# Starting the third layer before the feed-forward layer has finished its last groups

## The reference, cut to what matters

```
x = x + conv_0(group_norm(x)); x = x + conv_1(group_norm(x))
t = tokens(x)                              # 16 images x 256 tokens x 96 channels
t = t + causal_attention_2(layer_norm(t))  # "layer 2": 6 heads of 16
t = t + bit_ffn(layer_norm(t))             # two sign-weight matmuls, 96 -> 384 -> 96
t = t + causal_attention_3(layer_norm(t))  # "layer 3", with biases
t = t + mixture_of_experts(layer_norm(t))  # 4 experts, top 2
```

## Time and profile before

| | us |
|---|---|
| median of 3 runs | 800.56 (797.04 to 800.75) |
| the profiled execution | 800.84 |
| its span | 798.6 |

### The profile page before, as it was taken

One profiled execution on the slowest core, in us unless ns is written; L12 is line 12 of the kernel. 1 busy time (PEld: TensorE's weight loads), 2 busy tenths in 40 slices (PEclk: granted clock), 3 DMA queues, 4 the chain that ended last, 5 costly groups with the idle time before them and its releaser, 6 DMA issues.

```text
span 798.6 us, 16946 instructions
## 1 busy us (share of the span) xinstructions
PE 739.9 (93%) x5265; PEld 579.9 (73%) x5265; DVE 582.8 (73%) x1415; ACT 570.7 (71%) x1425; POOL 252.8 (32%) x485
## 2 busy tenths in 40 slices
PE   1896999999999888999998987899999999999997
PEld 1874788787788776777776586677777787777775
DVE  6238677676777566888787698688887836988885
ACT  3323787877777556888887775688888847787785
POOL 1902255565554342122121100031221210534434
PEclk9999999999999999999999998899999989999999
DMA  6000000110110132323331002133233102322220
GB/s 219 1 1 0 1 7 17 21 16 17 21 16 16 24 91 66 101 81 104 91 92 29 0 1 69 52 97 103 79 104 92 41 1 55 78 65 74 60 50 21
DMA packets 60073, 41.36 MB, mean 52 GB/s; under 512 B 33904, under 2 KB 52464, under 8 KB 59888
## 3 DMA queue, kind: packets, MB, share of 16 engines
q1 hardware_dynamic: 60016, 40.63, 20.0%
HBM read 12.24 MB, written 3.21 MB: 19 GB/s over the span
## 4 chain that ended last, share of the span: by engine, by line
PE 78%; DVE 11%; ACT 4%; issue 3%; DMA 2%; SPq 1%; POOL 1%; POOLq 0%; DVEq 0%
PE ps L1248 11%; PE ps L992 10%; PE ps L1426 8%; PE ps L1183 8%; PE ps L1093 6%; PE ps L997 5%; PE ps L1077 3%; PE ps L1021 3%; PE ps L1035 3%; PE ps L1000 2%; PE ps L1022 2%; PE ps L942 2%; DVE amax L1867 2%; PE ps L1065 2%; DMA qk<-hl 1%
## 5 line engine op out<-in xcount | busy, mean ns | idle before, releaser
L627 ACT ACTIVATE ee<-ps,nmax 128x128 f32<-128x128 f32 (+1 forms) x576 | 204.7, 444 | 11.6 <-DVE nmax L1597 6.4
L1248 PE MATMUL ps<-w,ee 128*128 128x128 f32 x960 | 134.4, 273 | 2.0 <-ACT big L614 1.9
L1248 PEld LDWEIGHTS ps<-w,ee 128*128 128x128 f32 x960 | 112.4, 142 | 13.6 <-ACT ee L627 2.8
L614 ACT ACTIVATE big<-ps 128x512 f32<-128x512 f32 (+1 forms) x192 | 96.5, 554 | 24.3 <-PE ps L1248 22.4
L1600 DVE TENSOR_REDUCE nmax<-ps 128x2 f32<-128x256 f32 x192 | 97.5, 550 | 13.1 <-PE ps L1000 8.5
L1721 DVE TENSOR_TENSOR hhl<-ee,hhl 128x512 fp32r<-128x512 f32 x96 | 77.3, 815 | 26.2 <-ACT hhl L861 24.7
L992 PE MATMUL ps<-kh,big 128*128 128x256 f32 x384 | 94.7, 391 | 1.5 <-POOL big L387 1.2
L1597 DVE TENSOR_REDUCE nmax<-ps 128x4 f32<-128x1024 f32 x48 | 58.7, 1224 | 45.0 <-PE ps L992 44.8
L1426 PE MATMUL ps<-hhl,w2hl 128*96 128x512 f32 x288 | 83.3, 399 | 2.1 <-issue 1.8
L1183 PE MATMUL ps<-qk,w1hl 128*128 128x512 f32 x288 | 84.4, 402 | 0.0
L531 POOL TENSOR_TENSOR xc<-big,xc 96x512 f32<-96x512 f32 x32 | 52.9, 1655 | 95.2 <-DVE big L1952 94.6
(11 more groups left out here) (260 smaller groups left out, 1331.0 us busy)
## 6 DMA issues: line engine op xcount, KB each, us to landing
qk<-hl SPq DMA_DIRECT2D x256, 96.0 KB, 3.1
big<-moe_gate SPq DMA_DIRECT2D x8, 768.0 KB, 6.9
w<-w_in SPq DMA_DIRECT2D x1, 1735.0 KB, 12.3
xc<-x_in SPq DMA_DIRECT2D x4, 384.0 KB, 5.6
l_mix<-on SPq DMA_DIRECT2D x32, 48.0 KB, 2.1
tok<-l_mix SPq DMA_DIRECT2D x16, 96.0 KB, 2.0
out<-xc SPq DMA_DIRECT2D x8, 192.0 KB, 2.1
w<-w_in SPq DMA_DIRECT2D x1, 998.0 KB, 8.8
```

The source lines that it names most:

```text
L614: nc.scalar.activation(et[:, h, 0:w], ps[:, 4 + hh, 0:w], ACT.Copy).then_inc(own(l, f"et{hh}"), 1)
L627: last = nc.scalar.activation(ee[:, ke, hh, qc, 0:w], src, ACT.Exp, bias=nmax[:, kp, hh, qc:qc + 1])
L1248: last = nc.tensor.transpose(ps[:, 4 + hh, b * P:(b + 1) * P], ee[:, u, hh, qc, tc * P:(tc + 1) * P], ident)
```

## The change

- The lists are cut. `F2_PE`, `F2_ACT` and `F2_DVE` end earlier; what is left of groups 2, 3 and 4 moves into layer 3's written-out units, by tables: `F2_LATE_PE` (transposes 2 to 7 in units 0, 1, 5, 8, 11, 14), `F2_LATE_ACT` (their copies in the same units; roots 3, 4; normalising of groups 2, 3 in units 0 and 3), `F2_LATE_DVE` (`f` of groups 3 and 4 in units 0 and 1, `b` of group 3, `n` of group 4). POOL gets its own list, `F2_POOL`, with its maxima in the same order.
- Transposes and their copies no longer go by group in two halves but by four tiles (two images), T0 to T7, all into bank 6 (the first into bank 0), and layer 3 waits for each where it needs it: units 3, 6, 9, 12, 15 hold the weighing until a copy is done. POOL's staging and its other weights are put in a new order.
- On TensorE, `Q0` no longer follows all of the third group's matmul, `S0` waits for no later group's sums, and `Y2_BANKS` gives the second matmul ten uses of eight banks, so that groups 2 and 3 wait for no sum.
- Image 0's stacking is shared: SyncE issues four of its eight DMAs, ScalarE the other four (step `D0`).
- Layers 2 and 3 both lose the dummy image: for image -1 each step is only an increment of its semaphore. The matmuls L1194 and L1327 go too.
- In layer 3 six images are written out instead of two; the loop starts at image 6.

```diff
-F2_PE = [..., "y3", "T0", "Q0", "y4", "T1", "Q1", "S0", "T2", "S1", "T3", "V0", "T4"]
-F2_ACT = [..., "L0", "R0", "N0", "R1", "C0", "N1", "Q0", "R2", "N2", "C1", "Q1", "R3", "N3", "C2", "R4", "X0", "C3", "C4"]
-F2_DVE = [..., "y2", "b1", "f2", "k0", "y3", "b2", "f3", "y4", "k1", "b3", "m0", "f4", "n4", "m1", "v0"]
-Y2_BANKS = [(6, 7), (0, 1), (6, 2), (0, 1), (6, 2)]
+F2_PE = [..., "y3", "T0", "Q0", "y4", "Q1", "S0", "T1", "S1", "V0"]
+F2_ACT = [..., "L0", "R0", "N0", "C0", "Q0", "R1", "D0", "N1", "Q1", "R2", "X0", "C1"]
+F2_DVE = [..., "y2", "k0", "b1", "f2", "y3", "m0", "k1", "b2", "y4", "m1", "v0"]
+F2_LATE_PE = {0: [2], 1: [3], 5: [4], 8: [5], 11: [6], 14: [7]}
+F2_LATE_ACT = {0: ["C2", "N2"], 1: ["C3", "R3"], 2: ["R4"], 3: ["N3"], 5: ["C4"], 8: ["C5"], 11: ["C6"], 14: ["C7"]}
+F2_LATE_DVE = {0: ["f3"], 1: ["f4"], 2: ["b3"], 3: ["n4"]}
+Y2_BANKS = [(6, 7), (0, 1), (2, 3), (4, 5), (6, 3)]
...
-            def ln3_transposes(g):
+            def ln3_transposes(m):
+                g = (2 * m + 1) // GI
...
+                if m == 0:
+                    pe.wait_ge(sg("f2_y2"), 4)
+                elif m == 1:
+                    pe.wait_ge(sg("f2_y2"), 2 * NG)
+                else:
+                    pe.wait_ge(sg("l3_xn"), m)
+                for t in range(4):
+                    last = nc.tensor.transpose(ps[0:C, ln3_bank(m), t * P:(t + 1) * P], on[:, 4 * m + t, :], ident)
+                last.then_inc(sg("ln3_t_ps"), 1)
...
+                        elif step[0] == "D":
+                            act.wait_ge(*upto(3, "hi", g + 1))
+                            for t, (h0, h1) in enumerate(((0, 0), (0, 1), (1, 0), (1, 1))):
+                                if t == 1:
+                                    act.wait_ge(*upto(3, "lo", g + 1))
+                                parts = hl[C // 2:C, g, :, :, :].rearrange("c a h x -> c (a h) x")[:, h0:h1 + 3:h1 + 2 - h0, :]
+                                nc.scalar.dma_start(qk[(4 + t) * HD:(5 + t) * HD, g, 3:9, :].bitcast(F32), parts.bitcast(F32)).then_inc(own(3, f"stacked{g}"), 16)
...
@@ TensorE, unit @@
+                    if l == 3 and isinstance(k, int) and k in (3, 6, 9, 12, 15):
+                        pe.wait_ge(sg("l3_xn"), k // 3 + 3)
...
-                        weigh_values(l, npar, 0)
-                        weigh_values(l, npar, 1).then_inc(own(l, "av"), 1)
+                        if isinstance(i, int) and i == 0:
+                            pe.sem_inc(own(l, "av"), 1)
+                        else:
+                            weigh_values(l, npar, 0)
+                            weigh_values(l, npar, 1).then_inc(own(l, "av"), 1)
...
+                    if l == 3 and isinstance(k, int):
+                        for m in F2_LATE_PE.get(k, []):
+                            ln3_transposes(m)
...
-                for i in range(B if l == 1 else 2):
+                for i in range((0, B, 2, 6)[l]):
...
@@ VectorE, unit @@
+                    if l == 3 and isinstance(k, int):
+                        for step in F2_LATE_DVE.get(k, []):
+                            feed_step(step)
@@ TensorE, second matmul @@
-                                if g >= 2:
-                                    pe.wait_ge(sg("f2_y2"), 2 * (g - 2) + b + 1)
+                                if g == NG - 1:
+                                    pe.wait_ge(sg("f2_y2"), 1 if b == 0 else 6)
```

More of the change, by code:

```diff
@@ L307, in stack @@
                     parts = hl[:, par, :, :, :].rearrange("c a h x -> c (a h) x")[:, h0:h1 + 3:h1 + 2 - h0, :]
-                    for hh in range(2):
+                    for hh in sides:
                         r0 = hh * 4 * HD + t * HD
@@ L320, in _ @@
             for l in (2, 3):
-                stack(l, 0, 0)
-                stack(l, 1, 1)
+                for n in range(2):
+                    stack(l, n, n, (0,) if l == 3 and n == 0 else (0, 1))
                 if l == 2:
@@ L660, in outputs_to_sbuf @@
             def outputs_to_sbuf(l, i):
+                if isinstance(i, int) and i < 0:
+                    act.sem_inc(own(l, "ot"), 1)
+                    return
                 act.wait_ge(*upto(l, "av", i + 2))
@@ L670, in outputs_by_channel @@
             def outputs_by_channel(l, i):
+                if isinstance(i, int) and i < 0:
+                    act.sem_inc(own(l, "oc"), 1)
+                    return
                 act.wait_ge(*upto(l, "oc_ps", i + 2))
@@ L736, in inverse_root, with late @@
                     nc.scalar.activation(rs, rs, ACT.Exp, scale=-0.5).then_inc(sg("l1_rs"), 1)
+            def late(k):
+                for step in F2_LATE_ACT.get(k, []):
+                    g = int(step[1:])
+                    if step[0] == "R":
+                        ln3_root(g)
+                    elif step[0] == "N":
+                        ln3_norm(g)
+                    else:
+                        ln3_channels(g)
             for l in (1, 2, 3):
@@ L1038, in outputs @@
             def outputs(l, i):
+                if isinstance(i, int) and i < 0:
+                    pe.sem_inc(own(l, "oq"), 1)
+                    return
                 pe.wait_ge(*upto(l, "ot", i + 2))
@@ L1047, in outputs_back @@
             def outputs_back(l, i):
+                if isinstance(i, int) and i < 0:
+                    pe.sem_inc(own(l, "oc_ps"), 1)
+                    return
                 pe.wait_ge(*upto(l, "on", i + 2))
@@ L1061, in project_outputs @@
             def project_outputs(l, i):
+                if isinstance(i, int) and i < 0:
+                    pe.sem_inc(own(l, "out_ps"), 1)
+                    return
                 pe.wait_ge(*upto(l, "oc", i + 2))
@@ L1631, in normalise_outputs @@
             def normalise_outputs(l, i):
+                if isinstance(i, int) and i < 0:
+                    dve.sem_inc(own(l, "orec"), 1)
+                    dve.sem_inc(own(l, "on"), 1)
+                    return
                 dve.wait_ge(*upto(l, "oq", i + 2))
@@ L1641, in add_outputs @@
             def add_outputs(l, i):
+                if isinstance(i, int) and i < 0:
+                    dve.sem_inc(own(l, "added"), 1)
+                    return
                 dve.wait_ge(*upto(l, "out_ps", i + 2))
@@ L1907, in _ @@
+                    for step in F2_DVE:
+                        feed_step(step)
             dve.wait_ge(sg("f3_gl_ps"), 8)
```

193 lines of the change are left out of this document (97 added, 96 removed).

## The result

| | before | after |
|---|---|---|
| median, same chip | 799.51 (796.37 to 802.67, 20 runs) | 803.54 (799.17 to 806.68, 20 runs) |
| the profiled execution, its span | 800.84, 798.6 | 804.32, 802.4 |

The ratio is 1.0046, 95% interval [1.0031, 1.0061]: 3.7 us slower (the medians differ by 4.0). The forecast was 798.0, with a range up to 801.8. One kernel's time goes with its clock: of the 20 executions after, the three shortest (799.2 to 799.5) have a mean granted clock of 0.972 to 0.977, the three longest (806.1 to 806.7) 0.962 to 0.964.

The account below looks back on a forecast made before the run. TensorE bounds layer 3, DVE is late in the seam before it. Gains 8.5 - 2.0 - 1.3 = 5.2, less 3.0 for the clock, plus 0.5 in layer 2, make 2.7 off: 798 (797.9), range 794.8 to 801.8.

Parts of the forecast that it names:

- Step 1: Group 3's second matmul follows group 2's directly, with no sum to wait for, ending about 477.4; nothing uses this alone.
- Step 2: Image 0's path from transposes through DMAs shared by two issuing engines: scores 0 at 488.7, before 495.38.
- Steps 3 and 4: DVE's queue up to image 0's weighing, with `f4` at 3.8: weighing 0 at 507.4 instead of 515.94, 8.5 gained.
- Step 5: Image 1, with group 3's normalising and `n4` ahead: weighing 1 comes 10.3 after weighing 0, not 8.3; 2.0 lost.
- Step 6: Late transposes of units 8, 11 and 14 each add 0.45 on a TensorE without idle: 1.3 lost.
- The clock: Half-clock stretches behind TensorE's idles in the seam into layer 3 add 4.2; 3.0 taken, bounds 0 and 6.
- Rival B: In the seam one or no fall of the clock hits the path: 4.7 to 6.7 gained, 794 to 796; chance 0.30.
- Layer 2: Without the dummy image's matmuls, image 2's projection can start earlier: 0.5 gained, bounds 0 and 1.5.
- Rival C: Units 0 to 5: work put into images 0 and 1 costs more than the seam gave; 805; chance 0.08.

Follow-up runs that it names:

- old_fresh_bank: The kernel before with only the fresh bank, so group 3's second matmul waits for no sum: 798.27, ratio 0.9999.
- best: Changed kernel with idle transposes (26 ahead of weighing 0), tiny early GpSimd operation, GpSimd's weights later, `n4` and `N3` ahead of their engines' waits: 792.51, ratio 0.9932.
- warm_slots: Changed kernel with idle transposes in four TensorE waits and `n4` and `N3` moved to where their engines wait anyway: 795.63, ratio 0.9961.
- warm: Changed kernel with idle transposes put into four TensorE waits, the last 34 ahead of weighing 0: 798.18, ratio 0.9982.
- slots: Changed kernel with DVE's `n4` and ScalarE's `N3` moved ahead of work for which their engines wait anyway: 800.28, ratio 1.0012.
- dummy2_back: Changed kernel with the dummy image and the matmuls L1327 restored in layer 2 alone: 804.97, ratio 1.0077.
- late_weights: Changed kernel with GpSimd preparing the second expert weights after image 2's copy, behind image 0's normalising: 808.61, ratio 1.0117.
- quiet: Changed kernel with a tiny GpSimd tensor_tensor behind image 2's copy and the second expert weights behind image 0's normalising: 800.10, ratio 1.0026.
- warm_quiet: Changed kernel with idle transposes in four TensorE waits, a tiny early GpSimd operation and GpSimd's weights later: 798.19, ratio 0.9996.
- sync_stacks: Changed kernel with SyncE issuing all eight DMAs of image 0's stacking and ScalarE none: 804.53, ratio 1.0073.
- spread: Changed kernel with the late DVE and ScalarE pieces laid thinner over more images: 810.71, ratio 1.0150.

## Why the prediction was wrong

The forecast had weighing 6 at 563.8 (566.0, less 5.2 at full clock, plus 3.0 of clock); it came at 569.22, 5.4 later. Three terms of its sum failed: the price of `f4`, the landing of the DMAs, and the discount on the clock. By its own steps:

- **Step 1** was right: group 3's matmul follows without a wait and ends at 477.1 (forecast 477.4), and `old_fresh_bank` shows no gain from it alone that its runs could tell.
- **Step 2** was right up to the DMAs (transposes 479.38 against 479.5, low part 483.2 against 483.1) and 1.3 late at scores 0 (489.96 against 488.7). The failed term is "lands 4.0 after its issue", taken from a row with one queue at work. That 4.0 runs from the start of the issue; in the same terms it took 5.77 with two queues (484.15 to 489.92), 5.12 of it the transfer, where the row of before had 3.38. ScalarE's own issues cost 0.67 each, near the 0.6 that I had.
- **Steps 3 and 4**: I had weighing 0 at 507.4 at full clock. `best` has it at 72.78 behind layer 2, which would be 509.0 in the trace of after: 1.6 later, and scores 0 were 1.3 late already. The step that failed is "`f4` (3.8)". Its price is from a row in which nothing ran on GpSimd beside it. In the new place it meets the weights and takes 5.6 (505.97 to 511.53), 1.8 more. From `best` to `warm_slots`, where the block is in and holds the scaling for 2.88, weighing 0 moves by 2.5. I had looked at GpSimd's list for its order, not for what its work does to DVE beside it. No rival held this.
- **Step 5** was right at full clock: 10.3 forecast, 10.63 in `warm`. But I took the 2.0 as a price to pay. `slots` and `warm_slots` show that it was a question of place: DVE and ScalarE had idle time just ahead, and with the clock up the gap falls to 8.77.
- **Step 6** was right, and a little high: weighing 1 to 6 takes 42.81 against 41.87 before, 0.9 where 1.35 was forecast.
- **The clock.** The list gave 4.2 and I took 3.0, since "which idle meets a fall can vary". From `after` to `warm`, weighing 0 moves by 1.4 and the gap by 2.7: 4.1. In `warm` the block is 0.7 longer, though. By `after`'s own rows weighing 0 stands 4.1 behind `best`'s place, 1.9 of it the block (the next operation is 0.1 longer too), so that 2.2 are the clock's, and 4.9 with the gap. The discount was wrong, and the sum of the list about right, but not its places: it had 2.5 ahead of weighing 0 and 1.7 behind. The 1.1 for projection 0 did not strike in this execution and did in seven others, so that the sum fits this trace is in part luck. The idle ahead of scores 0, forecast at 1.6, was 3.24, since the DMAs landed late. Rival B, the clock staying up, had 0.30 and was off altogether, with 0.57 over the 12 us from 488. The prediction also says that the stretches of the earlier trace rows agree with a rule on bursts shorter than the waits. They show a low clock behind each wait, but TensorE had been at work for longer than the wait ahead of each: over 7 us ahead of the 2.80, over 6 ahead of the 3.88, and about 5 ahead of the 3.26.
- **Layer 2** had 0.5 of gain. In the profiled execution layer 2's last weighing comes 0.13 earlier than before; in most others the gain is about 1, as said under `dummy2_back`.

Summed for weighing 6, by `after`'s own rows: start of image 0 at full clock 1.6 late, the block 1.9, the clock 1.9 (4.9 less the 3.0 taken), the gap 0.3, step 6 -0.4: 5.3 of 5.4. Beyond it 0.4 for layer 2 and 0.6 behind image 6, which is inside what executions differ by there.

Rival C had named the place, units 0 to 5, and its mark of weighing 6 past 567 was met. Its mechanism was so in part only: `slots` shows that the late lumps did hold image 1, for 3.0. But weighing 1 came at 526.41, not after 528, image 1 took 13.33, not 15, ScalarE's issues cost 0.67, not 1.0, and neither the block nor the longer landing was in it. The fault in the chances was that a moved block of 7 us on the latest engine got 0.08 for costing more in its new place than its row said.

## What to carry to other kernels

A duration from a row holds for the neighbours that it had there: before moving DVE work, look what GpSimd does in the new place. Late work that was moved into a busy phase cost about its length here, from image to image too, until it was put just ahead of a wait of its own engine; read those waits from the timeline first. An order that starts earlier with short bursts can give its gain back to TensorE's clock: take the idles that the laid-out queues show without a discount, or fill them. And one profiled execution is one draw: lay several traces side by side before a term of 1 us is called right or wrong.

## What the runs showed of the hardware

- **GpSimd pauses about 7 us ahead of the first TENSOR_TENSOR after a PARTITION_ALL_REDUCE**, once, without an instruction in the trace: 7.09 before, 7.01 after, 6.79 in `late_weights`, 6.99 in `quiet` and 7.52 in `warm_quiet`, the last two on 12 columns, and 6.79 to 7.52 in all fifteen kernels. COPY and CAST between them are not held. In layer 2 of the kernel before, with no PARTITION_ALL_REDUCE ahead, a TENSOR_TENSOR follows its CAST within 0.1 (301.10 to 301.19). The Trainium skill, "GPSIMD Engine Reference", section "2.1 Instruction dispatch", has the first call to a freshly loaded kernel pay about 6 us for loading its code, with nothing to be seen in a profile; the traces agree in kind and are 0.8 to 1.5 higher; that this pause is such a load, no run here shows.
- **Some DVE operations that overlap a GpSimd one are held until that ends.** The 128x576 TENSOR_SCALAR took 1.55 to 2.98 beside GpSimd's TENSOR_TENSOR of 2.6, and 0.52 without it. In six kernels (`after`, `sync_stacks`, `dummy2_back`, `slots`, `warm`, `warm_slots`) it starts 0.04 ahead of GpSimd's to 1.38 behind it, and always ends 0.31 to 0.33 after GpSimd's end. The SCALAR_TENSOR_TENSOR on the same tile took 3.06 in `spread` and 0.76 without. Others are not held: beside the same GpSimd operation in the kernel before (521.57 to 524.19) DVE's TENSOR_REDUCE and COPY from `ps` take their usual 1.01 and 0.35, and BATCH_NORM_STATS2 on `tok` its 0.42. In that place it cost nothing. The Trainium skill, "SBUF — State Buffer", section "Who interferes with whom", has both kinds wait until the other's end, as they share a pair of ports; the trace agrees, as the TENSOR_SCALAR ends 0.3 behind GpSimd's operation, whose own 2.62 is as long as where no DVE operation is held (2.64 in `best`). That section gives the ports to whichever starts first; in `warm` DVE's row starts 0.04 ahead of GpSimd's and is held all the same, which is too little to decide on, as GpSimd's spans are rough.
- **Two issuing queues for one stacking**: the DMA share was 0.98 in the 4.5 us with them, and 2.25 less at the issue gave 0.6 at the landing; the last transfer took 5.12 in `after` and up to 6.01 in `spread`, against 3.44 with one queue in `sync_stacks`.
